# A graph network on one core: TensorE's signals in the edge passes are raised by a drain behind each group of products instead of by the group's last product

## The reference, cut to what matters

```
# layer 0: weighted sum          layer 1: edge network, repeated twice
out = segment_sum(x[src] * ew * weight, dst)      W = (relu(attr @ w1 + b1) @ w2 + b2).reshape(E, 16, 16)
x = clip(x + out + x * self_loop_weight, 0, 1)    hx = gru(segment_sum(einsum('ei,eio->eo', hx[src], W), dst) / deg, hx)
# layer 2: attention, two layers  layer 3: one weight matrix per edge type, two layers
p = exp(leaky(a_s[src] + a_d[dst]) - max)         s_r = segment_sum(x[src] * (edge_type == r), dst)
out = segment_sum(h[src] * p / z, dst)            out = x @ root + bias + sum_r (s_r / cnt_r) @ W[r]
```

## Time and profile before

| | |
|---|---|
| median of 3 runs, us | 22,244.42 |
| span of the profiled execution, us | 30,666.4 |
| PE busy in it, us (share) | 19,689.1 (64%) |
| DVE busy | 18,344.5 (60%) |
| POOL busy | 16,237.0 (53%) |
| ACT busy | 2,899.0 (9%) |
| TensorE clock granted, mean | 0.798 |

### The profile page before, as it was taken

One profiled execution on the slowest core, in us unless ns is written; L12 is line 12 of the kernel. 1 busy time (PEld: TensorE's weight loads), 2 busy tenths in 40 slices (PEclk: granted clock), 3 DMA queues, 4 the chain that ended last, 5 costly groups with the idle time before them and its releaser, 6 DMA issues.

```text
span 30666.4 us, 276253 instructions
## 1 busy us (share of the span) xinstructions
PE 19689.1 (64%) x89726; PEld 9475.3 (31%) x89726; DVE 18344.5 (60%) x38447; ACT 2899.0 (9%) x6609; POOL 16237.0 (53%) x16846
## 2 busy tenths in 40 slices
PE   4466657767567776455555477777566665777775
PEld 1122223333223333233333233333333333333332
DVE  6566657777567777456666465555455554555554
ACT  3344400000000000100000000000000000000000
POOL 5555555555455555445555555555355554454555
PEclk8788878888778888677777688888688886888887
DMA  3333322222122222133333122222233332222221
GB/s 122 83 103 104 101 52 66 68 66 66 45 62 68 66 68 67 32 85 88 85 86 91 45 77 76 76 76 76 62 93 93 93 91 66 55 55 55 56 56 44
DMA packets 1271680, 2237.21 MB, mean 73 GB/s; under 512 B 386665, under 2 KB 737274, under 8 KB 1261818
## 3 DMA queue, kind: packets, MB, share of 16 engines
q1 hardware_dynamic: 729380, 2025.85, 19.9%
q0 software_dynamic: 538944, 192.26, 6.7%
q10 hardware_dynamic: 1942, 1.43, 0.0%
HBM read 1597.46 MB, written 620.66 MB: 72 GB/s over the span
## 4 chain that ended last, share of the span: by engine, by line
DVE 36%; another core or an unknown queue 27%; PE 22%; DVEq 7%; issue 7%; POOL 1%; DMA 0%; ACT 0%; ACTq 0%; SPq 0%; POOLq 0%
PE psB L768 17%; DVE Sb L1284 6%; DVE xT L1164 5%; DVE prod L1325 5%; DVE xT L1160 4%; DVE sub L1170 4%; DVEq L1169 3%; PE psB L839 2%; DVE prod L1328 1%; DVEq L1193 1%; DVE arena L1131 1%; DVEq L1324 1%; PE psB L905 1%; PE psA L799 1%
## 5 line engine op out<-in xcount | busy, mean ns | idle before, releaser
L768 PE MATMUL psB<-xp,arena 128*128 128x476 bf16 x26040 | 6949.8, 421 | 3618.6 <-DVE xT L1164 2521.8
L768 PEld LDWEIGHTS psB<-xp,arena 128*128 128x128 bf16 x26040 | 2630.0, 108 | 7599.1 <-issue 5550.5
L768 PE MATMUL psB<-ext,arena 128*128 128x308 bf16 (+1 forms) x17388 | 3670.7, 366 | 1826.4 <-issue 1114.7
L1160 DVE TENSOR_TENSOR xT<-psB,XT 128x616 bf16<-128x616 f32 (+1 forms) x1860 | 1803.2, 977 | 3128.9 <-remote 2508.0
L532 POOL DMA_INDIRECT gb<-tab3b,typi x2356 | 2269.1, 963 | 2348.7 <-DVE xT L1160 1489.5
L532 POOL DMA_INDIRECT gb<-tab1b,srci x2356 | 2293.3, 973 | 1929.0 <-issue 645.4
L532 POOL DMA_INDIRECT gb<-tab1a,srci x2356 | 2297.1, 975 | 1905.3 <-issue 651.3
L532 POOL DMA_INDIRECT gb<-tab2a,srci x2232 | 2111.8, 946 | 2047.6 <-DVE xT L1160 1350.0
L532 POOL DMA_INDIRECT gb<-tab2b,srci x2356 | 2229.3, 946 | 1789.9 <-DVE xT L1160 1043.6
L1164 DVE TENSOR_TENSOR xT<-psB,sub 128x476 bf16<-128x476 f32 x2976 | 1920.1, 646 | 2039.8 <-remote 1670.1
L532 POOL DMA_INDIRECT gb<-tab3a,typi x2108 | 2093.8, 993 | 1897.2 <-DVE xT L1164 1015.9
(11 more groups left out here) (337 smaller groups left out, 19385.5 us busy)
## 6 DMA issues: line engine op xcount, KB each, us to landing
arena<-oh_d SPq DMA_DIRECT2D x1861, 448.0 KB
hid<-oh_d SPq DMA_DIRECT2D x639, 448.0 KB
oh_d<-arena SPq DMA_DIRECT2D x558, 448.0 KB
ext<-oh_d SPq DMA_DIRECT2D x290, 448.0 KB
S2a<-Sb SPq DMA_DIRECT2D x62, 1404.0 KB
S2b<-Sb SPq DMA_DIRECT2D x62, 884.0 KB
ext<-in_attrT SPq DMA_DIRECT2D x404, 128.0 KB
S3a<-Sb SPq DMA_DIRECT2D x62, 832.0 KB
```

Source lines behind the costliest of these rows:

```text
L768: m = pe.matmul(psB[b][:, o:o + W], pk.onehot(n)[:, g, u * P:(u + 1) * P], pk.part(g, q).bitcast(BF16), start=g == 0, stop=g == NB - 1)
L1160: v.tensor_tensor(to.rearrange("p (b f x) -> p b f x", b=2, x=2 * JB), psB[b][:, :].rearrange("p (b w) -> p b w", b=2)[:, :, 0:W].rearrang ...
```

## The change

In the seven passes the semaphore increment is taken off the last product of each group and put on a drain of TensorE that follows the group. It concerns t_pick, t_typed, t_turn, t_hidden and t_weight. The products, their order and all waits stay; the stages on the nodes keep their signals on the products.

```
-                        m = pe.matmul(psB[b][:, o:o + W], pk.onehot(n)[:, g, u * P:(u + 1) * P], pk.part(g, q).bitcast(BF16),
-                                      start=g == 0, stop=g == NB - 1)
-                return m
+                        pe.matmul(psB[b][:, o:o + W], pk.onehot(n)[:, g, u * P:(u + 1) * P], pk.part(g, q).bitcast(BF16),
+                                  start=g == 0, stop=g == NB - 1)
...
-                pick_words(pk, n, u).then_inc(t_pick, 1)
+                pick_words(pk, n, u)
+                pe.drain().then_inc(t_pick, 1)
...
-                    t = pe.matmul(outs[u], pk.xT[0:K, o + u * P:o + (u + 1) * P], pk.mats, start=True, stop=True)
-                t.then_inc(t_typed, 1)
+                    pe.matmul(outs[u], pk.xT[0:K, o + u * P:o + (u + 1) * P], pk.mats, start=True, stop=True)
+                pe.drain().then_inc(t_typed, 1)
...
-                pe.transpose(psA[0][0:K, P:2 * P], pk.extra[:, o + K:o + 2 * K], ident).then_inc(t_turn, 1)
+                pe.transpose(psA[0][0:K, P:2 * P], pk.extra[:, o + K:o + 2 * K], ident)
+                pe.drain().then_inc(t_turn, 1)
...
-                        m = pe.matmul(psA[u][:, :], w1s[32 * u:32 * u + 26, :], atts[q % 3][32 * u:32 * u + 26, :], start=True, stop=True)
-                    m.then_inc(t_hidden, 1)
+                        pe.matmul(psA[u][:, :], w1s[32 * u:32 * u + 26, :], atts[q % 3][32 * u:32 * u + 26, :], start=True, stop=True)
+                    pe.drain().then_inc(t_hidden, 1)
...
-                            m = pe.matmul(psB[g % 2][:, to:to + 256], hid[64 * u:64 * u + 64, o:o + P],
+                            pe.matmul(psB[g % 2][:, to:to + 256], hid[64 * u:64 * u + 64, o:o + P],
                                           w2as[64 * u:64 * u + 64, 256 * u:256 * u + 256], start=True, stop=True)
-                    m.then_inc(t_weight, 1)
+                    pe.drain().then_inc(t_weight, 1)
```

## The result

| | before | after |
|---|---|---|
| median, us | 22,242.68 (4 runs, 22,240.15 to 22,245.08) | 22,875.89 (4 runs, 22,861.23 to 22,898.43) |
| ratio, 95% interval | | 1.0285 (1.0273 to 1.0297) |
| span of the profiled execution, us | 30,666.4; a second one 22,263.7 | 22,875.6 |

The change costs 633 us; 632 had been forecast, 22,880 against 22,875.89. That agreement is in part luck: passes 1 and 2 were priced 178 us too high, pass 6 was priced 91 and pass 5 78 us too low, as the experiments show, and these errors cancel.

A forecast was written before the change was run, and what follows sets the result against it. The kernel was taken to run near the largest of three engines in every pass: GpSimd, or VectorE in passes 1 and 2. Added costs of 384 + 186 + 31 + 31 = 632 us gave 22,880 us, range 22,400 to 23,600.

The forecast's parts named there:

- The unprofiled time from three engines' work per chunk: Largest of GpSimd, VectorE and TensorE per pass, together 323.5 us, times 62 chunks 20,060 us; 2,184 us left for the rest.
- Overlap lost: At each drain TensorE's next group no longer starts before the last ends: 0.07 or 0.16 us by place.
- The handoff: From a drain's end to TensorE's next first product: 0.15 us taken, bounded by 0 and 0.30.
- The later signals: Signals to other engines come some 0.1 us later, hidden by the buffers where TensorE isn't the bound.
- Pass 6: TensorE rises from 46.3 to 53.7 us a chunk against GpSimd's 47.5 and becomes the bound: 384 us.
- Pass 5: 36 drains bring TensorE to 42.0 us a chunk against 42.5; 0.5 a chunk for coupling, 31 us.
- Passes 1 and 2: TensorE at 49.3 us a chunk against VectorE's 50.5; nearly equal steps lose 1.5 a chunk, 186 us.
- Passes 0, 3 and 4: GpSimd's gathers hide the drains: nothing in passes 0 and 3, 0.5 us a chunk or 31 us in pass 4.
- TensorE's slack takes it all: Rival: TensorE is the largest in no pass, so its slack absorbs the drains; 22,244 to 22,280 us; chance 6%.
- Only the overlap: Rival: handoff near 0, pass 6 pays 126 us, elsewhere nothing; 22,370 to 22,590 up to 0.07 handoff; chance 17%.
- Dear: Rival: handoff of 0.30 us, passes 6, 1, 2, 5 and 4 pay 1,640 us, 23,880; chance 12%.
- Signals come sooner: Rival: drain increments come in time, VectorE's waits at L1160 and L1164 shrink; 21,870 us at best; chance 3%.

The follow-up runs named there:

- again: The kernel before, unchanged, profiled a second time; span of that execution 22,263.7 us.
- twice: The changed kernel with two drains behind each group, the increment on the second; 23,283.86 us, ratio 1.0461.
- ahead: The changed kernel, but in passes 5 and 6 the next group's waits stand ahead of the drain; 22,511.61 us, ratio 1.0120.
- bare: The changed kernel with increments back on the last products, each followed by a drain without an increment; 22,807.18 us, ratio 1.0243.

## Why the prediction was right, and where it wasn't

**The unprofiled time from three engines' work per chunk** held. It gave 40.0, 50.5, 50.5, 45.0, 47.5, 42.5, 47.5 us; the clean trace of before has, as pass length over 61 distances, 43.9, 50.9, 50.9, 45.1, 47.2, 43.6, 47.0. Pass 0 is longer since the searches for the nodes' ends lie in some of its chunks, which in my sum went into the rest. The 2.2 us that I added in passes 1 and 2 to VectorE's 48.3 busy us a chunk, for short pauses between its instructions, stood on no row; "again" shows them: in the window 3190 to 6200 of pass 1, 59 chunks, VectorE is busy for 2827.9 us and idle for 182, 3.1 us a chunk, of which 2.2 are 1,477 pauses of 0.05 to 0.15 us each and 0.8 is waiting for TensorE's weights. Setting aside the first profile's waits, because VectorE's work alone forbade them, was the step on which everything stood, and the second profile confirms it.

**Overlap lost**: 0.07 and 0.16 us as read the earlier trace rows. In the trace after, the seven products of a pick of 476 columns take 1.57 us from first start to modelled end, and seven at 0.20 are 1.41: 0.16 beyond, as read before the change. From starts alone only overlap and handoff together can be read: pick to pick takes 3.22 us in pass 6 after, against 14 x 0.20 = 2.81, which is 0.41 more. Without a handoff pass 6 would have paid 126 us by the prediction's sum, a quarter of its 475.

**The handoff** was the term that was mis-sized: 0.15 taken, between 0 and 0.30, and 0.23 measured. The reference I chose, TensorE resuming after a wait for VectorE, holds one wait that it already stood at. In the changed kernel two waits stand behind most drains, and the run with the waits ahead shows what that place costs: 0.08 to 0.09 us of handoff there, below my value, and 0.23 in the changed kernel, above it. The later signals, put at some 0.1 us in the prediction, are 0.02 us later.

**Pass 6**: 384 forecast, 475 measured. The handoff made a pair 7.95 instead of 7.67 us, which is 1.9 us a chunk or 120 us more; some 30 less than that were measured, for the most part because the last two chunks, with hardly any picks left beside them, did not get longer (the last two distances are 48.4 and 6.1 us after, 41.5 and 18.4 before). **Pass 5**: 31 forecast, 109 measured: TensorE has 45.6 us a chunk instead of 42.0, 2.9 of it by the handoff and the rest by an overlap of 0.18 rather than 0.16 us a drain (the pair 5.06 - 3.42 = 1.64 us longer, 4 handoffs are 0.92), partly offset by the gathers of this pass at 1.29 us and not 1.25, so that it had started from 43.6 and not 42.5. **Passes 1 and 2**: 186 forecast, 8 measured. Here I had miscounted: 404 hidden groups over two passes of 62 chunks are 3.3 a chunk, not 6.5. TensorE had 38.5 us and not 41.9; even at the dearer handoff it has 13 x 1.36 + 14 x 1.80 + 3.3 x 1.35 = 47.3, with the distances of the rows below, 3 us under the 50.3 of the shortest chunks there (5th percentile; median 50.8). The same holds inside the loop over groups, where the prediction looked for the loss: with a quarter of a hidden group per step and not half, TensorE needs 1.36 + 0.97 x 1.80 + 0.34 = 3.44 us a step against VectorE's 3.5, so the loss of 1.5 us a chunk had no cause. TensorE in pass 2 of the changed kernel:

```profile
6805.44 1.57 PE L768 MATMUL psB<-xp,arena 128*128 128x476 bf16 x7 [0.23 <-issue]
6807.24 1.14 PE L840 MATMUL psB<-w2as,hid 64*128 64x256 f32 x8 [0.23 <-issue]
6808.60 1.56 PE L768 MATMUL psB<-xp,arena 128*128 128x476 bf16 x7 [0.23 <-issue]
6810.40 1.13 PE L828 MATMUL psA<-ext,w1s 26*128 26x512 f32 x4 [0.23 <-issue]
6811.75 1.14 PE L840 MATMUL psB<-w2as,hid 64*128 64x256 f32 x8 [0.23 <-issue]
```

**Passes 0, 3 and 4** were hidden by GpSimd's gathers as said: 15 us measured, 31 forecast for pass 4, where TensorE's 47.2 us come close to GpSimd's 47.5.

**The rivals.** "TensorE's slack takes it all" is true of five passes and false of the two that count. "Only the overlap" would be 22,370 to 22,590; with the waits ahead the kernel comes into that range, at 22,512. "Dear", with 0.30, is what two drains give, though at 23,284 and not 23,880, as passes 1 and 2 had the room that the miscount had hidden. "Signals come sooner" fell: they come 0.02 us later, and putting them back on the products gained 69 us (22,807 against 22,876).

## What to carry to other kernels

Work out, per stage, the time of each engine from rows in stretches without a wait, and price a change of one engine against its distance to the largest: here 28 drains a chunk cost 8 us where TensorE stood 1 us below GpSimd, and 30 cost nothing where it stood far enough below VectorE. Keep TensorE's increments on its products: moving them to 10,820 drains cost 633 us here. Where a drain can't be avoided, put the next group's waits ahead of it, which took the handoff from 0.23 to 0.08 or 0.09 us, but only where those waits don't depend, directly or through another engine, on the signal of this very drain (that nothing would move on then is my conclusion from the order of the code; no run tried it); and count how often a group runs per stage from its total before multiplying.

## What the runs showed of the hardware that was not expected

A profiled execution of one and the same program took 30,666 us once and 22,264 us another time, with the same instructions; in the longer one busy shares were 19 to 27% lower (TensorE 64% and 79%, GpSimd 53% and 73%) and VectorE's waits for releases with no place came to thousands of us. The one profile by itself didn't tell such waits from the kernel's own; that VectorE's busy time left no room for them in the unprofiled 22,244 us did.

A second drain of TensorE directly behind the first cost 0.07 us ("twice", 0.301 against 0.229 in the medians of pass 5), and the waits of a group, two as a rule, cost 0.14 to 0.15 us more behind a drain than ahead of it ("after" 0.23, "ahead" 0.08 to 0.09). With the increment on a drain VectorE started 0.02 us later than with the increment on the last product (0.06 against 0.04 us behind the modelled end of the pick, "after" and "bare").

TensorE's mean granted clock was higher with drains than without, 0.941 against 0.903. The windows of pass 5 show 1.00 and 0.92 (length, busy us, clock, DMA; after, then "again"):

```profile
16380.00:19030.00 2650.00, 2157.82 (x10415) 1013.78 (x10415) 2063.48 (x5674) 315.72 (x1041) 1957.13 (x1969) 1.00 0.43 122
```

```profile
16380.00:18900.00 2520.00, 1965.56 (x10316) 1134.05 (x10314) 2013.99 (x5616) 313.68 (x1031) 1926.23 (x1948) 0.92 0.44 127
```

In the changed kernel TensorE sets the pace there and pauses 0.23 us at a time; before, it got ahead and then stood still for longer, in 15 of its 115 pauses ahead of a pick in that window for over 7 us. The clock was the higher there and the time was lost all the same. In pass 6 the windows of both traces show 1.00, so the clock has no part in what that pass lost.
